# Two layers of attention and feed-forward on one core: a table built between weight splits, smaller register loads, and earlier statistics with later keys in layer 1

## What is computed

```
x = x + tanh(g_xattn[0]) * L0_xattn(layernorm(x), ctx, ctx, Wq, Wk, Wv)     # one head, decay mask, rotary factors
x = x + tanh(g_ffn[0])   * L0_ffn(layernorm(x), ...)                        # 32 routed experts, 6 per token, + shared
x = x + tanh(g_xattn[1]) * L1_xattn(layernorm(x), ctx, ctx, wq, ..., bo)    # 16 heads of 16, softmax
x = x + tanh(g_ffn[1])   * L1_ffn(layernorm(x), W_fc, W_proj)               # relu^2, then 5 spiking steps

# inside L0_ffn
scores = sigmoid(x @ gate_w.T); topk_idx, topk_w = group-limited top 6 of 32
h = relu(einsum('th,eih->tei', x, up_w)) ** 2 * combine[:, :, None]
moe_out = einsum('tei,ehi->th', h, down_w)
```

## Time and profile before

| | us |
|---|---|
| time before, median of 3 runs (1312.7 to 1321.49) | 1320.06 |
| the profiled execution, its own time | 1323.86 |
| its span (first to last instruction) | 1322.1 |
| PE busy | 1026.5 (78%) |
| DVE busy | 862.7 (65%) |
| ACT busy | 641.4 (49%) |
| POOL busy | 619.7 (47%) |
| DMA moved in the span | 188.26 MB, mean 142 GB/s |

### The profile page before, as it was taken

The page is one execution under the profiler, slowest core; times in us unless marked ns, Lnnn a source line. Parts: engine busy times, 40 slices in busy tenths (PEclk is TensorE's granted clock), DMA queues, the critical chain, the costliest instruction groups (busy, mean ns, idle before and its releaser), DMA issues.

```text
span 1322.1 us, 26576 instructions
## 1 busy us (share of the span) xinstructions
PE 1026.5 (78%) x8609; PEld 705.9 (53%) x8609; DVE 862.7 (65%) x1995; ACT 641.4 (49%) x1130; POOL 619.7 (47%) x889
## 2 busy tenths in 40 slices
PE   4998898888715888889634466988988888899886
PEld 2655565555404878788611223555555554566564
DVE  3775666666653666776645654767868686888654
ACT  2332333333433667677511253665656665676762
POOL 0156786778982112111188888084655647000000
PEclk9999999998756999999957677998989898999997
DMA  8343553323236888798664475354555546111110
GB/s 306 134 158 132 197 222 129 124 102 110 106 119 189 267 277 283 237 299 281 222 171 139 79 152 84 92 97 102 113 100 119 96 100 111 51 51 51 43 34 16
DMA packets 125428, 188.26 MB, mean 142 GB/s; under 512 B 21872, under 2 KB 98288, under 8 KB 124784
## 3 DMA queue, kind: packets, MB, share of 16 engines
q1 hardware_dynamic: 93040, 133.06, 31.4%
q0 software_dynamic: 32256, 53.50, 17.4%
HBM read 98.15 MB, written 75.24 MB: 131 GB/s over the span
## 4 chain that ended last, share of the span: by engine, by line
POOL 15%; PE 14%; issue 8%; DVE 7%; ACT 2%; DMA 2%; SPq 1%; DVEq 1%; POOLq 0%; ACTq 0%
POOL x_tok L2004 12%; PE bank L348 7%; PE bank L1631 3%; DVE row_max L1881 3%; PE bank L1587 1%; SPq L1436 1%; DMA inverse<-den_mid 1%; PE bank L1545 1%; PE bank L1568 1%; DVEq L1946 1%; ACT hid L1731 1%; DMA den_mid<-den_inv 0%; POOL rstd L2036 0%; ACT prob L1707 0%; DVE spikes L1947 0%
## 5 line engine op out<-in xcount | busy, mean ns | idle before, releaser
L2004 POOL DMA_INDIRECT x_tok<-ys,y_row x144 | 233.5, 1621 | 42.4 <-issue 42.4
L1881 DVE TENSOR_REDUCE row_max<-bank 128x2 f32<-128x512 f32 x256 | 164.1, 683 | 38.4 <-PE bank L1545 31.7
L1707 ACT ACTIVATE prob<-bank 128x512 f32<-128x512 f32 x256 | 137.7, 590 | 81.3 <-PE bank L1568 63.7
L1007 POOL DMA_INDIRECT xs<-w_hi,slot_row x144 | 146.4, 1016 | 61.9 <-DVE slot_row L894 39.6
L1276 POOL COPY row_share<-row_tile 128x1 f32 x224 | 41.4, 233 | 196.4 <-DMA row_tile<-xs 168.7
L2040 POOL TENSOR_TENSOR rstd_f<-var_eps_f,minus_half 128x2 f32<-128x2 f32 x16 | 14.3, 897 | 218.8 <-DVE var_eps_f L1775 218.8
L1545 PE MATMUL bank<-k_stack,q_stack 48*128 48x256 f16 x512 | 55.2, 296 | 71.6 <-DVE row_max L1881 65.5
L1631 PE MATMUL bank<-w_hi,hid_half 128*128 128x256 f16 x512 | 95.5, 275 | 0.2 <-DVE hid_half L1936 0.2
L1115 PE MATMUL bank<-ident,row_tile 128*128 128x128 f16 x896 | 62.2, 225 | 39.8 <-issue 24.2
L348 PE MATMUL bank<-xt_tile,w_routed 128*128 128x128 f16 x1344 | 88.8, 223 | 0.0
L1162 ACT ACTIVATE xt_tile<-bank 128x1024 f16<-128x1024 f16 x56 | 57.4, 1025 | 55.6 <-PE bank L1115 54.5
(11 more groups left out here) (236 smaller groups left out, 2565.1 us busy)
## 6 DMA issues: line engine op xcount, KB each, us to landing
row_tile<-xs SPq DMA_DIRECT2D x224, 144.0 KB, 3.2
ys<-y_tile SPq DMA_DIRECT2D x56, 512.0 KB, 4.2
w_routed<-in_weights_r SPq DMA_DIRECT2D x4, 2048.0 KB
inverse<-den_mid SPq DMA_DIRECT2D x64, 128.0 KB
xs<-zeros SPq DMA_DIRECT2D x32, 144.0 KB, 3.3
ctx_t<-in_ctx SPq DMA_DIRECT2D x8, 512.0 KB
ct_mid<-ct SPq DMA_DIRECT2D x8, 512.0 KB
ct<-ct_mid SPq DMA_DIRECT2D x8, 512.0 KB
```

The source lines that it names most:

```text
L1007: nc.gpsimd.indirect_dma_start(xs[:, :], bass.IndirectOffsetOnAxis(slot_row[p][:, tt, k:k + 1], axis=0), x_whole[g % 3][:, tt, :], None) \
L1707: nc.scalar.activation(prob[:, h % NPR, :, :], seconds.bank((n, h))[:, :], ACT.Exp, scale=float(HD) ** -0.5).then_inc(seconds.reader((n, h ...
L1881: V.tensor_reduce(row_max[n % PAIR][:, :, m, j], firsts.bank((n, 2 * j + m))[:, :].rearrange("p (q k) -> p q k", q=2), AX_X, ALU.max).then ...
L2004: nc.gpsimd.indirect_dma_start(x_tok[g % NXT][:, tt, :], None, ys[:, :], bass.IndirectOffsetOnAxis(y_row[:, g * TT + tt, k:k + 1], axis=0) ...
```

## The change

Five edits:

1. Block 1: the three parts of building the table become side steps at slots TABLE_AT, + 3 and + 9, between the splits. TABLE_AT is X_OUT_AT - TURN + LAST_STEP + 2 = 93 - 36 + 3 + 2 = 62.
2. Block 1: the last group's sends have no `rest` behind them.
3. Block 2: registers are loaded four at a time, once per pair; PE keeps three sets. SP loads its first before it waits for the sends.
4. Block 3: the statistics of x stand at slots 6, 7.5 and 7.8 instead of 11, 13.4 and 13.6, and power_x at 8.5 instead of 12; group 1 keeps its slots.
5. Block 3: k0 and k1 move from slots 4 and 7 to 10 and 12.

```diff
+            TABLE_AT = X_OUT_AT - TURN + LAST_STEP + 2
...
-                turns(dve, steps_dve, [(LAST_STEP * e + 1, low_routed, e) for e in range(EXPERTS)])
-                lay_out(count_tiles())
+                table_steps = [(TABLE_AT, count_tiles), (TABLE_AT + LAST_STEP, lay_out, tiles[1][:, 16:]),
+                               (TABLE_AT + 3 * LAST_STEP, table_row)]
+                turns(dve, steps_dve, [(LAST_STEP * e + 1, low_routed, e) for e in range(EXPERTS)] + table_steps)
...
-                    rest((g * TT + tt) * TOP_K + k)
+                    if g < GROUPS - 1:
+                        rest((g * TT + tt) * TOP_K + k)
...
-            def entries(eng, row, batch, sets, most):
-                at = batch * BATCH_TILES
-                eng.reg_load(sets[batch % 2], tab_row[0:1, row, at:at + BATCH_TILES])
-                return [eng.snap(r, min_val=0, max_val=most) for r in sets[batch % 2]]
+            def entries(eng, row, n, sets, most):
+                own = sets[n % len(sets)]
+                eng.reg_load(own, tab_row[0:1, row, 4 * n:4 * n + 4])
+                return [eng.snap(r, min_val=0, max_val=most) for r in own]
...
+                sp.wait_ge(tab_in, 1)
+                row_of = entries(sp, 0, 0, sets, EXPERTS * ROOM - TILE)
                 for r in range(3):
                     sp.wait_ge(sent[r], SENT * len(range(r, GROUPS, 3)))
-                sp.wait_ge(tab_in, 1)
-                row_of = []
...
-                        if 4 * n % BATCH_TILES == 0:
-                            col_of += entries(pe, 1, 4 * n // BATCH_TILES, sets, (EXPERTS - 1) * 2 * RCOLS)
+                        col_of += entries(pe, 1, n, sets, (EXPERTS - 1) * 2 * RCOLS)
...
-            FRONT = {"k0": 4, "k1": 7, "x0": 19, "x1": 21, "q0": 23, "q1": 25, "v0": 27, "v1": 29}
+            FRONT = {"k0": 10, "k1": 12, "x0": 19, "x1": 21, "q0": 23, "q1": 25, "v0": 27, "v1": 29}
...
+            stats_at = lambda g: (14, 16.4, 16.6) if g == 1 else (6, 7.5, 7.8)
+            power_at = lambda g: 15 if g == 1 else 8.5
...
-                    steps += ([(norm_at(g), moments_x), (norm_at(g) + 2.4, more_moments_x), (norm_at(g) + 2.6, last_moments_x),
+                    steps += ([(at, step) for at, step in zip(stats_at(g), (moments_x, more_moments_x, last_moments_x))]
...
-                    steps = [(norm_at(g) + 1, power_x)]
+                    steps = [(power_at(g), power_x)]
```

More of the change, by code:

```diff
@@ L952, in count_tiles @@
                         dve.drain()
-                    return tiles[1][:, 16:]
                 def lay_out(ends):
@@ L976, in lay_out, with table_row @@
                     V.tensor_reduce(tab[:, :, 0], start_row[:, :, :], AX_X, ALU.add).then_inc(tabled, 1)
+                def table_row():
                     dve.wait_ge(tab_full, 1)
@@ L1043, in build @@
             LAG = 2
-            BATCH_TILES = 16
             up_bank, y_bank, turn_bank = psum[0:2], psum[2:6], psum[6:8]
@@ L1055, in build @@
             block = second.enter_context(nc.Block())
-            def entries(eng, row, batch, sets, most):
-                at = batch * BATCH_TILES
-                eng.reg_load(sets[batch % 2], tab_row[0:1, row, at:at + BATCH_TILES])
-                return [eng.snap(r, min_val=0, max_val=most) for r in sets[batch % 2]]
+            def entries(eng, row, n, sets, most):
+                own = sets[n % len(sets)]
+                eng.reg_load(own, tab_row[0:1, row, 4 * n:4 * n + 4])
+                return [eng.snap(r, min_val=0, max_val=most) for r in own]
             @block.sync
             def _(sp):
-                sets = [[sp.alloc_register(f"row{n}_{i}") for i in range(BATCH_TILES)] for n in range(2)]
+                sets = [[sp.alloc_register(f"row{n}_{i}") for i in range(4)] for n in range(2)]
                 n1 = STAGE[1]
+                sp.wait_ge(tab_in, 1)
+                row_of = entries(sp, 0, 0, sets, EXPERTS * ROOM - TILE)
                 for r in range(3):
                     sp.wait_ge(sent[r], SENT * len(range(r, GROUPS, 3)))
-                sp.wait_ge(tab_in, 1)
-                row_of = []
                 def store(n):
@@ L1081, in _ @@
                     if n < PAIRS:
-                        if 4 * n % BATCH_TILES == 0:
-                            row_of += entries(sp, 0, 4 * n // BATCH_TILES, sets, EXPERTS * ROOM - TILE)
+                        if n > 0:
+                            row_of += entries(sp, 0, n, sets, EXPERTS * ROOM - TILE)
                         wait(sp, rows_full[1], n - NR + 1)
@@ L1102, in _ @@
             def _(pe):
-                sets = [[pe.alloc_register(f"col{n}_{i}") for i in range(BATCH_TILES)] for n in range(2)]
+                sets = [[pe.alloc_register(f"col{n}_{i}") for i in range(4)] for n in range(LAG + 1)]
                 pe.wait_ge(tab_in, 1)
@@ L1265, in _ @@
             def _(pool):
-                sets = [[pool.alloc_register(f"expert{n}_{i}") for i in range(BATCH_TILES)] for n in range(2)]
+                sets = [[pool.alloc_register(f"expert{n}_{i}") for i in range(4)] for n in range(2)]
                 pool.wait_ge(tab_in, 1)
@@ L1269, in _ @@
                 for n in range(PAIRS):
-                    if 4 * n % BATCH_TILES == 0:
-                        expert_of += entries(pool, 2, 4 * n // BATCH_TILES, sets, EXPERTS - 1)
+                    expert_of += entries(pool, 2, n, sets, EXPERTS - 1)
                     pool.wait_ge(rows_loaded[n % NR], 64 * (n // NR + 1))
```

2 lines of the change are left out of this document (1 added, 1 removed).

## The result

| | us |
|---|---|
| before, median of 20 runs (1307.42 to 1326.79) | 1316.37 |
| changed, median of 20 runs (1299.9 to 1314.72) | 1308.78 |
| ratio, with its 95% interval | 0.9929 (0.9908 to 0.995) |
| forecast; range | 1288; 1264 to 1330 |

The change saves 0.7%: 9 us by the ratio, 7.6 by the two medians. The time lies in the range and on the side that I named, but the size failed: I had forecast over three times as much (-32 us). 0.7% lies within the 1% that I had called no difference, with a chance of 0.16.

The account below looks back on a forecast made before the run. PE was taken as the expert stage's bound, DMA close behind, and layer 1's POOL adds as holding the others; -3 -10 +7 -22.5 -5 = -33.5 from 1323.9 gave 1290.4, or 1286.6 by median; forecast 1288 us, range 1264 to 1330.

Parts of the forecast that it names:

- End of layer 0, -3: Block 1's end: sends without copies closer together, -2, and shorter first register loads, -1; the table's move at no cost.
- Loads of four, -10: Expert stage: loads of 0.67 us stall PE 0.43 each, 55 of them 23.7 us against 33.5 before, so -10.
- per-entry bound: Expert stage: if load time goes by entry, a load of four takes 0.47 us and the stage changes by -21.
- the floor of 600 ns: The skill's least time for a small register load; scaled to PE under traffic, the loads would cost 12 us.
- the unstalled pair of 3.55 us: Expert stage: spacing of two unstalled pairs on PE against 4.25 over 48 pairs, an excess of 33.5 us to win.
- My own formula: Expert stage: load time less 0.24 us hidden by the queue, times 55 loads, set against the excess of 33.5 us.
- Turn 2, +7: Layer 1: power_x ahead of four adds leaves POOL idle some 6.5 us, and 21 adds precede power_f instead of 17.
- The sign that I named: Layer 1, turn 2: a POOL gap of 6 to 7 us and xn_f's wait for power_f at 18 us.
- Turns 3 to 6, -22.5 for the statistics: Layer 1: earlier statistics let POOL's adds start sooner, removing xn_f's four waits, 22.5 us; bounds -24 and 0.
- -5 for the keys: Layer 1: keys' matmuls moved into PE's feed-forward waits gain some 40% of 13 us; bounds -13 and +8.
- The first rival: Expert stage: a large fixed part makes loads of four 0.85 us, the stage stays, about 1298 us; chance 0.22.
- the third rival: Layer 1 gives nothing, as a wait on row_max replaces xn_f's; -13 in all, about 1309 us; chance 0.17.

Follow-up runs that it names:

- power2_back: The changed kernel with power_x of turn 2 back at slot 12, so four adds stand ahead of it on POOL; 1293.3 us, ratio 0.983.
- keys_alone: The kernel before with only the keys' move to slots 10 and 12; 1314.7 us, ratio 0.995.
- stats_back: The changed kernel with statistics of x back at slots 11, 13.4, 13.6 and power_x at 12; 1311.7 us, ratio 0.996.
- before_again: The kernel before, unchanged, run and profiled once more; 1312.4 us in one run.
- fewer_adds_ahead: power2_back without the copies behind layer 1's first gathers and with six of turn 2's adds moved behind its first power_f; 1287.7 us, ratio 0.978.
- best: fewer_adds_ahead with register loads of eight entries once per two pairs on all three engines; 1302.6 us, ratio 0.985.

## Why the prediction was right or wrong

Means over the profiles that share a stretch's code sum to about the measured difference: end of block 1 (the seventh group's first send to the first turning of rows; three profiles against 14) 82.2 to 80.9, -1.3; E 244.0 (four profiles with loads of 16) to 246.9 (nine with four), +2.9; G 162.2 (two) to 170.6 (eight), +8.4; between the two power_f of turn 2, -0.9; T 282.8 (two) to 263.2 (eleven), -19.6; R 187.7 to 189.2, +1.5. That is -9.0, and (1 - 0.9929) x 1316.4 is 9.3. That the two agree so well is partly luck: ahead of these stretches the seventh group's first send came at 329.4 us in the mean of the three profiles and at 326.2 in the 14, though no edit reaches that part.

- **End of layer 0, -3: right in kind, the gain at most half.** The sends fell from 1.34 to 1.26 apart where they run free and kept the splits' 1.445, as said: 32.6 us for the 23 spacings against 33.0. Block 1 ended at 400.5 with DVE done at 383.1, so the table's move was free. Measured -1.3, which single profiles don't show clearly (81.4 to 82.6 us against 79.0 to 83.5).
- **Loads of four, -10: failed, and half of the miss is here; measured +2.9, which is nothing, by the 3 to 6 us between executions.** The load's price was below even my per-entry bound (0.33 us against 0.47; I took 0.67), and the floor of 600 ns that I cited from the Trainium skill (DMA: Bandwidth & Descriptors, Latency and other measured facts) is not there: the least load took 0.3. The step that failed is the one from a load to what it costs: I read the unstalled pair of 3.55 us as PE's pace alone and let 0.24 us of each load hide behind it. No row shows the 0.24; in the earlier trace rows the stall is as long as the load (2.84 us at a load of 2.86). The 3.55 is the sequencer's pace too, so a load costs its whole length and its register operation, 0.59 us: 55 x 0.59 = 32.5, against the 33.5 that 14 loads of 16 had cost. My own formula with that price gives -1. (It sets 55 loads against the excess of 48 pairs; over all 55 spacings a pair took 4.18 us in the mean before and 4.17 after.) What betrayed it in the trace of before was there: the loss per pair was larger than the stalls at L1115 (33.5 against 24.2 us), since the pair behind a stall was slow too (3.9 us).
- **Turn 2, +7: held.** The gap is 7.08 us. The sign that I named, xn_f's wait at 18 us, did not come: it grew only from 11.66 to 12.48, as DVE's own work ahead of it came later too (its wait began 157.4 us after the first gather, before at 151.4). G has the cost, +8.4, and power2_back, at 164.2, is 6.4 below their mean.
- **Turns 3 to 6, -22.5 for the statistics and -5 for the keys: the waits right, the sum counted twice.** The four waits of xn_f went, here and in the profiles of all twelve other kernels with early statistics. With the keys in their old place T fell by 23.5 us (282.8 to 259.3, two profiles each), with the keys moved by 19.6, not by 27.5. What failed is the keys' term as an addition: alone the keys gave some -5.5 in T (two profiles each), what I had put down for them, but out of the same waits (22.5 and 21.2 us before, 16.3 in keys_alone, 14.9 in stats_back), and beside the early statistics nothing was left for them to gain.
- **What the -22.5 was made of: partly luck.** I priced the waits alone. By the rows of the two profiles T lost 19.8 us, and 12 of them are PE's busy time (245.57 to 233.66 us for 2264 and 2258 matmuls), at a mean granted clock of 0.93 before and 0.98 after; only 8 are PE's idle time. Before, the clock fell to its lower level (1.2 GHz) right behind each of the four waits of xn_f, when PE had been nearly idle: busy 0.99 of 4.9, 0.28 of 3.5, 0.83 of 4.2 and 0.43 of 3.0 us. How much of the 12 us lay on the path, no run isolates. The last of these waits, in the columns of the earlier trace rows:

```profile
1101.50:1104.50 3.00, 0.43 (x8) 0.00 (x0) 0.82 (x3) 0.00 (x0) 2.82 (x3) 1.00 0.56 82
1104.50:1111.30 6.80, 5.47 (x29) 2.81 (x30) 5.70 (x12) 1.62 (x3) 5.88 (x4) 0.50 0.58 101
```

- **Where the sum was hung.** The profiled execution lay 7.5 us above the median of 20 runs, not 3.8 above; I went part of that way, 5 us too little. It hid some of the miss: 21 us in the time, 24 in the difference.

The first rival (the stage stays as it is: 1298) named the right outcome for the stage with the wrong reason, a load of 0.85 us. The measured 1308.8 is by chance the time of the third rival (1309), whose mechanism did not come: layer 1 did gain.

## What to carry to other kernels

Where an engine's instructions take addresses from registers, count what its sequencer does per step (here 24 operations of 0.124 us) before calling the engine the bound. Where the sequencer has no slack, a load or register operation costs its full length wherever it stands, and the gain lies in fewer address operations (without 18 of the 24 a pair took 3.54 us instead of 4.16). Before adding the gains of two edits, ask whether they take the same waits: here the two together gave no more than the larger alone. Ahead of an instruction that waits for a landing, leave work in the queue that can run meanwhile: moving it up put 7 us of idle time on POOL, and one number put back took another 1% (0.983 against 0.993).

## What the runs showed of the hardware

- A register load on PE takes 0.31 us for one entry, 0.33 for four, 0.59 for eight and 1.1 at the least for 16: a floor of 0.3 us that four entries reach, then 65 ns an entry.
- On PE's sequencer an address operation with its weight loads and matmuls went every 0.124 us; with 24 of them to 52 matmuls a pair took 3.55 us without a load, and 4.16 with one of four entries.
- Loads that began some 0.7 to 1.8 us after the issue of a store of 512 KB took up to three times as long (1.02 us against 0.32 for four entries on POOL, 1.47 against 0.59 for eight on PE); most between 1.1 and 1.8 us were longer than the least, and no run moves the store alone.
- Some 2260 matmuls of turns 3 to 6 kept PE busy 245.6 us at a mean granted clock of 0.93 and 230.5 to 237.6 us at 0.97 to 0.99.
- Two executions of one program differed by 6 us in one stretch (E, before and before_again), and one code of layer 1 by 13 us in G (fewer_adds_ahead and best). The medians of 10 and 20 runs of one program, taken beside different runs of the kernel before, differed by 5 us.
